# Fused convolution stack, KAN layer: two exponentials and six products a network, SiLU and variance root by ScalarE tables, one ring of bases, strided identity sum, another order

## The chip, the cores and the metric

One core of one Trainium2 chip runs the whole program in one launch. The metric is device time in microseconds. The program takes 10815.07 us (median of 3 runs, 10814.88 to 10825.75).

## The reference

Four layers are added to a tensor `x` of 8 x 32 x 256 x 256 f32, each on the group-normalized `x`: a hyperbolic convolution block, a spectral layer, a window layer of four KAN networks, and a local binary pattern. The change is in the third. Its reference, cut to what matters (`y` is the layer-normalized input; one set of 16 or 32 values is one row of a network):

```python
GRID, DENOM = jnp.linspace(-2.0, 2.0, 8), 4.0 / 7.0
def _fastkan(x, ln_g, ln_b, ws, wb, bb):
    ln = _layernorm(x, ln_g, ln_b)
    basis = jnp.exp(-((ln[..., None] - GRID) / DENOM) ** 2)      # 8 bases
    return basis.reshape(*basis.shape[:-2], -1) @ ws.T + jax.nn.silu(x) @ wb.T + bb
a = _fastkan(columns of windows of y, k1...)     # 16 values a row
d = _fastkan(rows of windows of y, k2...)        # 16 values a row
e = _fastkan(channels of y, k3...)               # 32 values a row
z = _fastkan(a + d + e, k4...)                   # 32 values a row
out = z + wins
```

## The kernel before

`build_program` runs the layers one after another; `window_layer` (from L1679) is the third, and `prepare_kan` prepares its constants. It works on 64 tiles of 128 partitions x 2048 f32, each half a band of eight rows of the images. The five normalizations are PN (of the input, L1991 and L1995 write `y`) and those of the networks K1 to K4.

A tile goes through these steps. Each normalization has three on TensorE, which share the four PSUM banks `norm`: `center` (L2115, L2118), `variance` (L2128, from the squares `sq`) and `spread` (L2139, which spreads the reciprocal roots). Between them ScalarE moves the centered values out of PSUM (L1863, L1865) and squares them (L1872), VectorE takes the variance (`take`, L1979) and works out the reciprocal root by a polynomial (`chain`, eight small steps in `rsqrt_polynomial`, L116 to L130; K1, K2 and K3 in one chain, PN and K4 in the other), and multiplies (`scale`, L1991).

A network's eight bases are exp(-(v + c - n)^2) up to a constant. ScalarE computes three of them (the anchors 0, 3 and 6) as a square (L1898, `args`) and an exponential (L1902, `exps`), and once a network the ratio exp(2v) (L1907, `ratio`). VectorE makes each of the other five from the base below it by one multiplication with the ratio (`grow`, L2042); the constant that is left over is multiplied into the weights `kan_basis`. Anchors lie in `ex` (three buffers), the others in `grown_ex` (three buffers). TensorE multiplies each base by its weights (`products`, L2180: 32 instructions, a matmul of f32 being two) and sums in the other four PSUM banks, `out`. Ahead of base 4 it adds the SiLU part (L2173), for K3 also the result of K1 through the identity (L2166), for K4 the residual (L2170). SiLU is x (1 + tanh(x/2)) / 2: Tanh on ScalarE (L1881, L1886), the rest on VectorE (L2000), the half in the weights.

`out` is evacuated by ScalarE for K1, K2 and K4 (L1912). For K3 VectorE adds `out`, the bias and the result of K2 into `z` (`total`, L2007); it reads `out` row by row while it lies column by column, and so with a stride. K1 and K2 get their inputs by DMA (`feed_y`, `feed_u`) and give back by DMA (`give_back`). For K2 the tile is first turned, columns first, by VectorE (`turn_y` L1958, `turn_u` L1963), with a stride of eight words on reading.

The order of the work is written out by hand: every step has a position (`CENTER`, `MOVE`, `GROW`, ... ), in units of which 128 make a round; position 168 is unit 40 of the round after the tile's own. Each engine goes through the units of all rounds and issues what is due, so that several tiles are in work at once, and waits on semaphores for what it needs. All rounds are unrolled. In a round the products of the networks come in the order K4, K1, K2, K3.

## Time and profile before

| | before |
|---|---|
| time, median of 3 runs | 10815.07 us |
| the profiled execution, its span | 10821.2 us |
| TensorE, VectorE, ScalarE busy, whole span | 8878.0, 8891.7, 8014.9 us |
| window layer, from the first `x` out of PSUM to the last `out` | 4403 to 10060 us |
| granted TensorE clock, mean | 0.936 |

The profiled execution's own time is its span, first to last instruction; no other time of it is given. The layers ahead of the window layer take about 4400 us, the one behind it about 750. A row of a group of instructions gives the busy time, the mean of one in ns, and behind the bar the idle time of the engine just before them with what ended it. Consecutive instructions overlap a little, so the start of the next one tells what one costs.

### The profile page before, as it was taken

How to read it: one execution, taken by the hardware profiler on the slowest of the kernel's cores; microseconds unless marked ns; L12 is line 12 of the kernel's file. 1: busy time of each engine (PE TensorE's matmuls, PEld its weight loads, DVE VectorE, ACT ScalarE, POOL GpSimd, SP SyncE). 2: the span in 40 equal slices, each digit the busy share in tenths (PEclk: the TensorE clock that was granted, in tenths of full speed). 3: DMA queues.
4: the chain of work that ended last, by engine and by line, in shares of the span. 5: the costliest groups of instructions: out<-in, count | busy, mean ns of one | idle time of the engine just before them, and what ended most of it. 6: DMA issues, size and time to landing. Idle time of an engine off the chain costs nothing. (4 is left out here: it accounts for less than half of the span.)

```text
span 10821.2 us, 354779 instructions
## 1 busy us (share of the span) xinstructions
PE 8878.0 (82%) x158376; PEld 4547.3 (42%) x158376; DVE 8891.7 (82%) x9022; ACT 8014.9 (74%) x5451; POOL 0.2 (0%) x4
## 2 busy tenths in 40 slices
PE   0889879996665799588888888888888888888788
PEld 0344434433442688244444444444344444443444
DVE  6777756666777588699999999999999999998788
ACT  0555545554552555599999999999999999998788
POOL 0000000000000000000000000000000000000000
PEclk9999989998887999699999999999999999999899
DMA  7999979996663588355444454555445455554576
GB/s 286 247 257 260 240 217 263 266 264 211 267 274 120 155 279 277 77 115 111 110 107 111 107 111 107 115 119 112 111 107 111 107 111 115 119 110 93 173 211 195
DMA packets 1196555, 1825.76 MB, mean 169 GB/s; under 512 B 135328, under 2 KB 956448, under 8 KB 1124768
## 3 DMA queue, kind: packets, MB, share of 16 engines
q1 hardware_dynamic: 1195040, 1803.05, 61.9%
q8 instruction: 1257, 20.59, 0.8%
q14 instruction: 258, 2.11, 0.1%
HBM read 717.78 MB, written 411.04 MB: 104 GB/s over the span
## 5 line engine op out<-in xcount | busy, mean ns | idle before, releaser
L2042 DVE SCALAR_TENSOR_TENSOR grown_ex<-ratio,ex 128x2048 f32<-128x2048 f32 x768 | 1756.1, 2287 | 229.7 <-PE out L2180 162.1
L2180 PE MATMUL out<-grown_ex,kan_basis 32*32 32x512 f32 x40960 | 1691.9, 625 | 7.7 <-DVE grown_ex L2042 5.4
L556 PE MATMUL conv<-uc,w 128*32 128x512 f32 x12288 | 1445.6, 596 | 15.4 <-DMA uc<-u 15.4
L1902 ACT ACTIVATE ex<-ex 128x2048 f32<-128x2048 f32 x768 | 1447.6, 1901 | 4.2
L2180 PE MATMUL out<-ex,kan_basis 32*32 32x512 f32 x24576 | 1233.3, 660 | 256.5 <-ACT ku L1912 156.5
L2042 DVE SCALAR_TENSOR_TENSOR grown_ex<-ratio,grown_ex 128x2048 f32<-128x2048 f32 x512 | 1171.2, 2288 | 27.4 <-PE out L2180 21.3
L463 ACT ACTIVATE v<-conv,cb 128x512 f32<-128x512 f32 x512 | 350.8, 685 | 899.6 <-PE conv L556 388.3
L2180 PEld LDWEIGHTS out<-grown_ex,kan_basis 32*32 32x32 f32 x40960 | 590.6, 106 | 731.1 <-issue 631.5
L1898 ACT ACTIVATE ex<-kin,offset 128x2048 f32<-128x2048 f32 x384 | 758.6, 1991 | 128.4 <-PE out L2180 127.8
L556 PEld LDWEIGHTS conv<-uc,w 128*32 128x32 f32 x12288 | 498.0, 109 | 715.7 <-issue 667.9
L2319 DVE TENSOR_TENSOR d<-xt 128x2313 f32<-128x2313 f32 (+2 forms) x256 | 621.7, 2495 | 88.2 <-PE acc L2373 87.9
L2373 PE MATMUL acc<-d,weights 32*32 32x512 f32 x16384 | 626.6, 599 | 73.3 <-issue 67.4
L2180 PEld LDWEIGHTS out<-ex,kan_basis 32*32 32x32 f32 x24576 | 419.6, 107 | 613.3 <-issue 532.5
L2139 PE MATMUL norm<-q,c_sel 32*128 32x128 f32 x10240 | 461.5, 328 | 171.5 <-ACT x L1863 136.6
L2139 PEld LDWEIGHTS norm<-q,c_sel 32*128 32x128 f32 x10240 | 391.8, 226 | 481.7 <-ACT x L1863 195.5
L2341 ACT ACTIVATE d<-d,steep 128x2313 f32<-128x2313 f32 (+2 forms) x256 | 534.0, 2159 | 35.3 <-DVE d L2319 35.3
L660 DVE TENSOR_TENSOR u<-xn,spread 128x512 f32<-128x512 f32 (+2 forms) x320 | 379.3, 1218 | 165.7 <-PE spread L521 163.5
L2128 PE MATMUL norm<-sq,c_kan_ones 128*32 128x128 f32 x10240 | 362.0, 281 | 176.3 <-ACT y L1865 76.0
L2173 PE MATMUL out<-ku,kan_silu 128*128 128x512 f32 x1024 | 472.6, 605 | 1.5 <-DVE grown_ex L2042 1.5
L2128 PEld LDWEIGHTS norm<-sq,c_kan_ones 128*32 128x32 f32 x10240 | 271.5, 112 | 464.8 <-issue 197.0
L2373 PEld LDWEIGHTS acc<-d,weights 32*32 32x32 f32 x16384 | 319.5, 103 | 327.7 <-issue 216.5
L1898 ACT ACTIVATE ex<-z,offset 128x2048 f32<-128x2048 f32 x192 | 383.2, 1996 | 54.5 <-PE out L2180 44.0
(287 smaller groups left out, 16012.2 us busy)
## 6 DMA issues: line engine op xcount, KB each, us to landing
uc<-u SPq DMA_DIRECT2D x2048, 129.0 KB, 3.5
xt<-in_x SPq DMA_DIRECT2D x128, 1024.0 KB, 7.3
t<-v SPq DMA_DIRECT2D x128, 1024.0 KB, 9.7
back_k<-ku SPq DMA_DIRECT2D x1024, 128.0 KB, 4.0
xt<-in_x SPq DMA_DIRECT2D x32, 2048.0 KB, 7.8
xt<-t SPq DMA_DIRECT2D x64, 1024.0 KB, 6.6
tt<-t SPq DMA_DIRECT2D x64, 1024.0 KB, 12.1
x<-x SPq DMA_DIRECT2D x64, 1024.0 KB, 4.9
```

What stands on the lines that cost most here:

```text
L556: last = m.matmul(conv[QUAD * b:QUAD * b + QUAD, k % 2, :], w_sb[:, o, d, :], uc[:, h, b, 2 * p:2 * p + 2, d:d + COLS], start=(d == 0), st ...
L660: return v.tensor_tensor(inside(u[:, h, first_row:first_row + rows, 1:COLS + 1]), inside(xn[:, h, at].rearrange("p (r w) -> p r w", w=COLS ...
L1898: a.activation(ex[:, j], norm_out(kind, h), ACT.Square, bias=k["offset"][:, kind - 1, n:n + 1]).then_inc(args, 1)
L1902: a.activation(ex[:, j], ex[:, j], ACT.Exp, scale=-1.0).then_inc(exps, 1)
L2042: v.scalar_tensor_tensor(grown_ex[:, at % GROWN], ratio[:], LARGEST, below, ALU.min, ALU.mult).then_inc(grown, 1)
L2128: last = m.matmul(norm[rows(quarter), 0, 0:P], k["c_kan_ones"][:, 0 if kind in (K1, K2) else 1, i, :], sq[:, block_:block_ + P], start=(i ...
L2139: last = m.matmul(norm[:, quarter, P * i:P * i + P], k["c_sel4"][rows(quarter), i, :], q[group][rows(quarter), group.index(kind), :], star ...
L2173: m.matmul(out[:, i, :], k["kan_silu"][:, kind - 1, :], silu_of(kind, h)[:, cols(i)], start=False, stop=False)
L2180: last = m.matmul(out[rows(i), g, :], k["kan_basis"][rows(g), kind - 1, n, :], base[rows(g), cols(i)], start=(n == 0), stop=(n == BASES - ...
L2319: v.tensor_tensor(d[:, h, n, rows, columns], there, xt[:, parity, h, rows, columns], ALU.subtract).then_inc(diff_ready, 1)
L2341: a.activation(t, t, ACT.Tanh, scale=steep[:, h:h + 1]).then_inc(tanh_ready, 1)
L2373: last = m.matmul(acc[quad(k), h, g, :], weights[quad(g), n, :], source_tile[quad(g), row + 2 * k:row + 2 * k + 2, column:column + COLS], ...
```

## The change

In the window layer alone:

- Two anchors a network, 0 and 4, instead of three; bases 1, 2, 3, 5, 6 and 7 come from products with the ratio, six instead of five.
- All eight bases of all networks go through one ring `ex` of six buffers, in order of use; a base may be written when the base six before it has been used by TensorE and the one above that has been made.
- SiLU by ScalarE's own function (`ACT.Silu`), whose table set is not that of the exponentials: `tables` loads a set where another one is active. VectorE's half of SiLU goes, and the factor one half in the weights.
- The reciprocal root as exp(-0.5 ln(v + eps)) on ScalarE, `log` reading the variance out of PSUM and `root` on 128 x 128 values, each network by itself. `take` and `chain` go.
- K2's result, not K1's, is added by the identity on TensorE, which reads it with a stride of 256 words; K1's result is added by VectorE at the evacuation of K3, which now reads `out` straight and writes `z` straight.
- SiLU(y) is turned by ScalarE (`TURN_U_BY_ACT`), the square of K3 goes to VectorE.
- Waits on constants in place of TensorE's counting registers; semaphores of `args`, `exps`, `ratios` and `grown` one for each network.
- Another order, in units of 256 to a round, with one round more of depth. The products come in the order K3, K1, K2, K4.

```diff
-ANCHORS = {K1: (0, 3, 6), K2: (0, 3, 6), K3: (0, 3, 6), K4: (0, 3, 6)}
-CHAINS = ((K1, K2, K3), (PN, K4))
-UNITS = 128
-STAGES = 4
+ANCHORS = (0, 4)
+GROWTHS = tuple(n for n in range(BASES) if n not in ANCHORS)
+EXP_SET, SILU_SET = "natural_log_exp_and_others", "silu_and_others"
+UNITS = 256
+CENTER = {PN: 437, K1: 727, K2: 749, K3: 732, K4: 1179}
+VARIANCE = {PN: 462, K1: 746, K2: 818, K3: 758, K4: 1216}
+SPREAD = {PN: 589, K1: 761, K2: 920, K3: 785, K4: 1223}
+EVACUATE = {K1: 922, K2: 1014, K3: 1040, K4: 1365}
+RATIO = {K1: 872, K2: 908, K3: 1065, K4: 1252}
+ANCHOR = {K1: (858, 875), K2: (883, 919), K3: (1060, 1099), K4: (1191, 1307)}
+EXP = {K1: (865, 877), K2: (888, 924), K3: (1063, 1112), K4: (1214, 1310)}
+PRODUCT = {K1: (921, 922, 938, 948, 950, 953, 959, 963),
+           K2: (985, 986, 987, 989, 993, 1003, 1007, 1008),
+           K3: (1115, 1124, 1125, 1128, 1135, 1136, 1144, 1165),
+           K4: (1274, 1286, 1288, 1296, 1299, 1300, 1301, 1305)}
+SILU = {PN: 617, K4: 1132}
+TURN_Y_BY_ACT = False
+TURN_U_BY_ACT = True
+SQUARED_BY_ACT = (PN, K1, K2, K4)
+STAGES = 5
+RING = 6
...
+        def base_buffer(kind, n, t):
+            return ex[:, serial(kind, n, t) % RING]
+        def buffer_free(eng, kind, n, t):
+            due = serial(kind, n, t) - RING
+            if due >= 0:
+                kind_before, t_before = slot_no.items[due // BASES]
+                n_before = due % BASES
+                eng.wait_ge(used, due + 1)
+                if n_before + 1 in GROWTHS:
+                    eng.wait_ge(grown[kind_before], len(GROWTHS) * t_before + GROWTHS.index(n_before + 1) + 1)
...
+            def tables(name):
+                if loaded_set[0] != name:
+                    a.preload_act_table_set(name)
+                    loaded_set[0] = name
...
-                    a.activation(U[:, h], Y[:, h], ACT.Tanh, scale=0.5).then_inc(tanh_ready[kind], 1)
+                    tables(SILU_SET)
+                    a.activation(U[:, t % 2], Y[:, t % 2], ACT.Silu).then_inc(u_ready[kind], 1)
...
+            def log(kind, t):
+                wait_past(act, spread_ready[kind], t)
+                act.wait_ge(var_ready[kind], t + 1)
+                tables(EXP_SET)
+                a.activation(logs[:, kind], norm[:, 0, 0:P], ACT.Ln, bias=k["eps"][:, 0:1],
+                             scale=1.0 * G / P if kind in (K1, K2) else 0.5 * G / P).then_inc(var_taken[kind], 1)
+            def root(kind, t):
+                act.wait_ge(var_taken[kind], t + 1)
+                tables(EXP_SET)
+                a.activation(roots[:, kind], logs[:, kind], ACT.Exp, scale=-0.5).then_inc(factors[kind], 1)
...
-                v.scalar_tensor_tensor(rows_first(Z[:]), rows_first(out_flat), out_b(K3, h), columns_first(D[:]), ALU.add,
-                                       ALU.add).then_inc(summed, 1)
+                    v.scalar_tensor_tensor(Z[:], out_flat, out_b(kind, t % 2), B[:], ALU.add, ALU.add).then_inc(evacuated[kind], 1)
...
-                            m.matmul(out[:, i, :], c["ident"][:], B[:, cols(i)], start=False, stop=False)
+                    by_rows = D[:].rearrange("p (x rw) -> p rw x", x=BAND)
+                    for i in range(CHUNKS):
+                        m.matmul(out[:, i, :], c["ident"][:], by_rows[:, BANK // BAND * i:BANK // BAND * i + BANK // BAND, :],
+                                 start=False, stop=False)
```

## Rows read from the trace of the kernel before

**Rows 1.** The page's first part: busy us, share of the span, instructions.

```profile
span 10821.2 us, 354779 instructions
PE 8878.0 (82%) x158376; PEld 4547.3 (42%) x158376; DVE 8891.7 (82%) x9022; ACT 8014.9 (74%) x5451; POOL 0.2 (0%) x4
```

**Rows 2.** Busy time in 46 tiles of the window layer; columns stand first.

```profile
core 0: us, PE busy (x) PEld busy (x) DVE busy (x) ACT busy (x) POOL busy (x), PEclk, DMA share, GB/s
5575.60:9564.80 3989.20, 3474.44 (x72495) 1645.45 (x72478) 3693.55 (x2622) 3698.72 (x1979) 0.00 (x0) 0.95 0.50 111
```

**Rows 3.** Tile `z`: times min/median/max in ns, first and last start.

```profile
L2007 DVE SCALAR_TENSOR_TENSOR z<-out,kan_vec,back_k x64: 3893/3946/3999, 4535.0 to 9998.1; 128x2048 f32<-128x2048 f32 x64
```

**Rows 4.** VectorE's groups in those 46 tiles: busy us, mean ns | idle before, releaser.

```profile
L2042 DVE SCALAR_TENSOR_TENSOR grown_ex<-ratio,ex 128x2048 f32<-128x2048 f32 x552 | 1262.1, 2286 | 149.6 <-PE out L2180 121.0 <-ACT ex L1902 19.9 <-issue 8.5
L2007 DVE SCALAR_TENSOR_TENSOR z<-out,kan_vec,back_k 128x2048 f32<-128x2048 f32 x46 | 181.7, 3950 | 20.7 <-ACT ex L1902 15.1 <-DMA back_k<-ku 5.6
L1991 DVE SCALAR_TENSOR_TENSOR z<-z,kan_vec,norm 128x2048 f32<-128x2048 f32 x46 | 107.8, 2344 | 0.1
L2000 DVE SCALAR_TENSOR_TENSOR silu_y<-silu_y,y 128x2048 f32<-128x2048 f32 x46 | 105.2, 2287 | 0.0
L1963 DVE COPY columns_first<-silu_y 128x2048 f32<-128x2048 f32 x46 | 93.5, 2033 | 0.0
L1979 DVE TENSOR_SCALAR q<-norm 128x128 f32<-128x128 f32 x230 | 65.7, 286 | 43.8 <-PE norm L2128 43.6
L120 DVE TENSOR_TENSOR t<-t,q 128x384 f32<-128x384 f32 x46 | 25.7, 559 | 3.4
L120 DVE TENSOR_TENSOR t<-t,q 128x256 f32<-128x256 f32 x46 | 19.6, 425 | 3.5
L116 DVE TENSOR_SCALAR rstd<-q 128x384 int32<-128x384 int32 x46 | 16.6, 360 | 4.3
L116 DVE TENSOR_SCALAR rstd<-q 128x256 int32<-128x256 int32 x46 | 13.5, 294 | 4.3
```

**Rows 5.** A tensor-tensor difference of the last layer, 2056 to 2313 elements, VectorE.

```profile
L2319 DVE TENSOR_TENSOR d<-xt x256: 2290/2558/2573, 10091.0 to 10800.9; 128x2313 f32<-128x2313 f32 x128
```

**Rows 6.** TensorE's groups in those 46 tiles.

```profile
L2180 PE MATMUL out<-ex,kan_basis 32*32 32x512 f32 x17663 | 885.2, 658 | 169.3 <-ACT ku L1912 110.2 <-ACT x_to_x L1912 50.0 <-issue 7.8
L2166 PE MATMUL out<-back_k,c_ident 128*128 128x512 f32 x368 | 174.4, 617 | 3.5 <-issue 3.5
```

**Rows 7.** One tile in order of time: start us, us; VectorE, then ScalarE.

```profile
6019.09 2.29 DVE L2042 SCALAR_TENSOR_TENSOR grown_ex<-ratio,grown_ex 128x2048 f32<-128x2048 f32 x1
6021.30 2.29 DVE L2042 SCALAR_TENSOR_TENSOR grown_ex<-ratio,ex 128x2048 f32<-128x2048 f32 x1
6023.50 2.03 DVE L1963 COPY columns_first<-silu_y 128x2048 f32<-128x2048 f32 x1
...
6020.00 1.92 ACT L1902 ACTIVATE ex<-ex 128x2048 f32<-128x2048 f32 x1
6021.82 1.98 ACT L1898 ACTIVATE ex<-kin,offset 128x2048 f32<-128x2048 f32 x1
6023.71 1.98 ACT L1907 ACTIVATE ratio<-kin,ratio_b 128x2048 f32<-128x2048 f32 x1
```

**Rows 8.** ScalarE in earlier layers: a table load, and passes over 128 elements.

```profile
3774.11 1.28 ACT L1311 ACT_TABLE_LOAD   x1
3775.40 0.91 ACT L1311 ACTIVATE grow<-z,w 128x256 f32<-128x256 f32 x2
...
L1155 ACT ACTIVATE xs<-rows,tables x128: 482/497/512, 3517.0 to 3706.2; 128x128 f32<-128x128 f32 x128
...
L805 ACT ACTIVATE th<-n x32: 293/297/309, 2603.3 to 3319.5; 128x128 f32<-128x128 f32 x32
```

More of the change, by code:

```diff
@@ L1785, in _, with rounds @@
+                t = self.number + (unit - position) // UNITS
+                return t if 0 <= t < TILES else None
+        def rounds(round_):
+            for n in range(TILES + STAGES):
+                round_(Round(n))
         @block.sync
@@ new lines, in exp, with growth @@
+            def exp(kind, j, t):
+                act.wait_ge(args[kind], len(ANCHORS) * t + j + 1)
+                tables(EXP_SET)
+                a.activation(base_buffer(kind, ANCHORS[j], t), base_buffer(kind, ANCHORS[j], t), ACT.Exp, scale=-1.0).then_inc(exps[kind], 1)
+            def growth(kind, t):
+                act.wait_ge(scaled[kind], t + 1)
+                last = slot_no.before(kind, t)
+                if last is not None:
+                    act.wait_ge(grown[last[0]], len(GROWTHS) * last[1] + len(GROWTHS))
+                tables(EXP_SET)
+                a.activation(ratio[:], norm_out(kind, t % 2), ACT.Exp, bias=k["ratio_b"][:, kind - 1:kind], scale=2.0).then_inc(ratios[kind], 1)
@@ L1914, in round_, with evacuate @@
+            def evacuate(kind, t):
+                act.wait_ge(used, serial(kind, BASES, t))
+                dst = R[:] if kind == K4 else silu_of(kind, t % 2)
+                a.activation(dst, out_flat, ACT.Identity, bias=out_b(kind, t % 2)).then_inc(evacuated[kind], 1)
             def round_(now):
@@ new lines, in round_ @@
+                    for kind in NORMS:
+                        if kind in MOVED_BY_ACT and (t := now.due(u, MOVE[kind])) is not None:
+                            move(kind, t)
+                        if kind in SQUARED_BY_ACT and (t := now.due(u, SQUARE[kind])) is not None:
+                            square(kind, t)
+                        if (t := now.due(u, LOG[kind])) is not None:
+                            log(kind, t)
+                        if (t := now.due(u, ROOT[kind])) is not None:
+                            root(kind, t)
@@ new lines, in round_ @@
+                    for kind in KANS:
+                        if (t := now.due(u, RATIO[kind])) is not None:
+                            growth(kind, t)
+                        for j in range(len(ANCHORS)):
+                            if (t := now.due(u, ANCHOR[kind][j])) is not None:
+                                anchor(kind, j, t)
+                            if (t := now.due(u, EXP[kind][j])) is not None:
+                                exp(kind, j, t)
+                        if kind in EVACUATED_BY_ACT and (t := now.due(u, EVACUATE[kind])) is not None:
+                            evacuate(kind, t)
@@ L1945, in _ @@
+            rounds(round_)
         @block.vector
@@ L2076, in _ @@
-            rounds(dve, round_)
+                    for kind in NORMS:
+                        if kind not in MOVED_BY_ACT and (t := now.due(u, MOVE[kind])) is not None:
+                            move(kind, t)
+                        if kind not in SQUARED_BY_ACT and (t := now.due(u, SQUARE[kind])) is not None:
+                            square(kind, t)
+                        if (t := now.due(u, SCALE[kind])) is not None:
+                            scale(kind, t)
+                    for kind in KANS:
+                        if kind not in EVACUATED_BY_ACT and (t := now.due(u, EVACUATE[kind])) is not None:
+                            evacuate(kind, t)
@@ new lines, in round_ @@
+                    for kind in KANS:
+                        for n in GROWTHS:
+                            if (t := now.due(u, GROW[kind][n])) is not None:
+                                grow(kind, n, t)
+                    for position, by_act, step in ((TURN_Y, TURN_Y_BY_ACT, turn_y), (TURN_U, TURN_U_BY_ACT, turn_u), (BETA, False, add_beta), (MEASURE, False, measure)):
+                        if not by_act and (t := now.due(u, position)) is not None:
+                            step(t)
@@ L2078, in _ @@
+            rounds(round_)
         @block.tensor
```

507 lines of the change are left out of this document (175 added, 332 removed).

## The prediction, made before the changed kernel was run

> **What bounds the kernel now.** I read the first part of the page, then the busy time by stretches, then one tile of the window layer engine by engine. The page gives a span of 10821.2 us with TensorE, VectorE and ScalarE busy 82, 82 and 74% [rows 1]; that is an average over unlike stages. The change touches only the window layer, so I need that layer's own period. `z` is written once for each of the 64 tiles, at 4535.0 us first and 9998.1 us last [rows 3], so one tile takes 5463.1 / 63 = 86.72 us and the layer is about half the span. I took 46 tiles from its middle, 3989.2 us [rows 2]: VectorE is busy 3693.55 / 46 = 80.3 us a tile, ScalarE 80.4, TensorE 75.5. No engine is the bound alone. They stand 6.4, 6.3 and 11.2 us a tile, in an order written out by hand, and all three carry nearly the same load. DMA is busy half the time, and no stretch of it ends many waits.
>
> VectorE's 6.4 us of gaps are of two kinds. The 16 small steps of the two reciprocal-root chains each have a gap of 3.4 / 46 = 0.07 us ahead of them [rows 4], 1.2 us in all, which belongs to the chains. The rest, 5.2 us, are true waits; half of them (121.0 / 46 = 2.6 us) stand before a product with the ratio and end when TensorE has used the base whose buffer is wanted [rows 4]. TensorE's largest waits are for the evacuation of `out`, the one set of banks for sums, by ScalarE: (110.2 + 50.0) / 46 = 3.5 us a tile [rows 6].
>
> Spans in these rows overlap a little. A product with the ratio lasts 2.29 us, but the next work starts 2.20 us after it; an exponential costs 1.82 us of the engine and a square with a bias 1.89 [rows 7]. I count these steps, not the durations.
>
> **VectorE, a tile.** Gone are: the chain of three networks, six steps of 0.56 and two of 0.36 us (4.1), the chain of two, six of 0.43 and two of 0.29 (3.1), their 1.2 us of gaps, five readings of the variance of 0.29 (1.4), the two half-SiLU products (2 x 2.20 = 4.4) and the turning of SiLU(y), which goes to ScalarE (2.03 less the overlap, 1.95) [rows 4]. The third network's evacuation read PSUM with a stride and took 3.95 us; now it reads straight, as the scaling does at 2.34, so 1.6 goes [rows 4]. Added are four products with the ratio, one more in each network (4 x 2.20 = 8.8), and the third network's square. The nearest row for that is a tensor-tensor difference of 2056 elements in 2.29 us, the shortest there [rows 5], so 2.2. Sum: -4.1 -3.1 -1.2 -1.4 -4.4 -1.95 -1.6 +8.8 +2.2 = -6.75. VectorE was occupied for 80.3 + 1.2 = 81.5 us and comes to 74.75.
>
> **ScalarE, a tile.** Four squares with a bias and four exponentials go: 4 x 1.89 + 4 x 1.82 = 14.8; the third network's square goes, 1.8. The two Tanh become two SiLU of the same size, taken at nothing; no row has a SiLU, and a row of Tanh on 128 elements has the same form of cost as the others, so I see no reason for a change either way. SiLU(y) is now turned here with a stride of eight words. Bounds: 1.8 us, a plain pass, and 1.8 times 1.69, the ratio of VectorE's strided to its straight reading of PSUM (3.95 to 2.34), so 3.0. I take 1.9, since VectorE's strided pass over SBUF [rows 4] is no dearer than its other full passes. Five logarithms and five exponentials of 128 elements are new. The nearest rows are 0.30 us (Tanh, no operand for scale or bias) and 0.49 us (two such operands) [rows 8]; ten of them are 3.0 to 4.9, less overlaps, and I take 3.5. Last, tables. The SiLUs want one set, exponentials and logarithms another. In a round's order on ScalarE (positions modulo 256) the first network's ratio stands at 104, SiLU(y) at 105, a square at 107, SiLU(z) at 108, the next exponential at 109: the two SiLUs stand together, and there is one pair of loads a tile. A load takes 1.28 us, and the next instruction starts right behind it [rows 8], so 2.6 us a tile, 166 us in all. Sum: 80.4 -14.8 -1.8 +1.9 +3.5 +2.6 = 71.8 us.
>
> Rows 8 show no gap behind the load. The Trainium skill (ScalarE: Activation LUTs, What ACT_TABLE_LOAD costs) puts a switch at about 2.66 us, a drain included. By that figure, an estimate, ScalarE would stand at 74.5 us a tile, and would still not be the most loaded engine.
>
> **TensorE, a tile.** The same products run. The registers that counted what to wait for go; gaps with no releaser shown before base products are under 0.3 us a tile [rows 6], so I take nothing for them. The sum with the identity, eight instructions of 0.6 us that overlap to 174.4 / 46 = 3.8 us a tile [rows 6], now reads its operand with a stride of 256 words between columns. Bounds: nothing, and the 1.69 above, +2.6 us; doubled it would be +3.8. Below nothing it can't go, the columns are the same. I take nothing, because VectorE reads SBUF with a stride without loss, and TensorE's pass over 512 f32 columns is slow enough for it (3.8 us for eight). So TensorE stays at 75.5 us and becomes the most loaded engine by 0.8 us.
>
> **Waits.** Anchors and products now share one ring of six buffers instead of three and three, so every base waits until the base six before it has been used. Behind a product that waits for this on VectorE stand all its other steps, the third network's evacuation and the scalings among them; behind an anchor on ScalarE, the evacuations for which TensorE waits. The number of buffers is the same, so I keep VectorE's 5.2 us of waits. That gives 74.75 + 5.2 = 80.0 us a tile. It leaves TensorE only 4.5 us of waits where it has 11.2. The new order puts two, one, three and two steps of the normalizations between one network's last product and the next network's first, where the old one has one, one, two and two, so there is more to hide an evacuation behind; still, variance, root and spreading of each network remain a relay over the same banks. If TensorE kept two thirds of its waits, it would ask for 75.5 + 7.5 = 83.0. I take 81.4, between the two. SyncE's queue has the same transfers, and a tile is still far longer than their issue.
>
> **Sum.** 64 x (86.72 - 81.4) = 340 us less. The third network's sums are finished 2.36 rounds behind the first centering instead of 2.02, so filling the pipeline may take 0 to 20 us more; I take 10. The profiled execution spans 10821.2 us, 6 us above the median of the runs; so 10821.2 - 340 + 10 - 6 = 10485.
>
> **The rivals.**
> A. TensorE takes over. All else is as above, but TensorE keeps most of its waits: at 84 to 86 us a tile the time is 10650 to 10780, with 85 about 10720. For it: TensorE's waits are for steps of one or two microseconds on the others, whose duration the change leaves. Against it: the other engines have 6 to 9 us less to do, and are ready sooner.
> B. Slower. TensorE keeps all its 11.2 us and the strided identity sum is dear: 75.5 + 11.2 + 2.6 = 89.3 us a tile, 10821.2 + 165 + 10 - 6 = 10990; doubled, 11067. It decides from the point at which the price of the stride and TensorE's waits together pass 11.2 us.
> The Trainium skill (Advanced Engine Details and Errata, SBUF Cachelines) speaks for B: successive accesses that fall on different 16-byte lines of SBUF pay a penalty, and here each column does; no row of this case shows it for TensorE.
> C. The ring frees VectorE. If its 2.6 us of waits for used bases go, it needs 77.4 us a tile: 10821.2 - 596 + 10 - 6 = 10229. Against it: TensorE would have 1.9 us of waits left. Halfway to the forecast it gives about 10340.
> D. The tables are not held: the set is changed at every logarithm and at every exponential behind one. Five pairs of loads more are 13 us, ScalarE comes to 84.8, with its present 6.3 us of waits to 91.1 us a tile, and the time to 11105.
>
> **How the numbers follow.** Forecast (80 to 83.5 us a tile, 10395 to 10620): 0.58. A: 0.18. B: 0.13. C: 0.07. D: 0.02. The remaining 0.02 is a time within 0.2% of now; 0.2% is about what a measurement of this kernel can tell from no change. Faster is the forecast, A and C, 0.83; the same 0.02; slower 0.15. The range runs from C's halfway point, 10340, to 10880, where B is well begun; it leaves out about 0.05 below and 0.12 above.
>
> **What would show it.** In the middle of the layer VectorE should be busy 74 to 75 us a tile, ScalarE 71 to 73, TensorE 75 to 77 at a like clock; 128 table loads; the identity sum near 0.6 us an instruction, against 1.0 or more under B; a period of 81.4 us. Waits of VectorE for used bases well under 2.6 us mean C; a TensorE busy 75.5 with over 8 us of waits, A. I should be wrong most easily in the waits, which I carry over from another order.

## The result, and the profile after

The changed kernel takes 11002.12 us (median of 4 runs, 10986.19 to 11035.08) against 10814.97 us (10807.23 to 10825.75) for the kernel before: a ratio of 1.0173, with an interval of 1.0150 to 1.0196. It is slower by 1.7%, where 3.1% faster was forecast (10485 us), and it lies outside the range given (10340 to 10880). Rival B had 10990.

The page's first part of the kernel after:

```profile
span 10991.8 us, 350519 instructions
PE 9088.7 (83%) x158376; PEld 4584.7 (42%) x158376; DVE 8630.6 (79%) x7794; ACT 7545.8 (69%) x5712; POOL 0.2 (0%) x4
```

Against [rows 1], VectorE is busy 261 us less and ScalarE 469 us less; only TensorE has more, 211 us, with the same number of matmuls. The span grew by 170.6 us. Tile `z` of the kernel after (duration ns min/median/max, first and last start):

```profile
L1996 DVE SCALAR_TENSOR_TENSOR z<-out,kan_vec,back_k x64: 2350/2352/2352, 4558.6 to 10192.6; 128x2048 f32<-128x2048 f32 x64
```

So a tile takes (10192.6 - 4558.6) / 63 = 89.43 us, 2.71 more than by [rows 3], and 63 x 2.71 = 171 us is the whole of the loss in the span. Outside of it things cancel: the first `z` starts 23.6 us later than in [rows 3], and what follows the last one is 23.9 us shorter. Busy time of the engines in the middle of the layer, in the columns of [rows 2]:

```profile
5536.80:9667.60 4130.80, 3623.49 (x72500) 1689.81 (x72500) 3509.94 (x1748) 3356.49 (x2164) 0.00 (x0) 0.95 0.56 108
```

A share of this stretch times the period gives an engine's busy time a tile, and the rest of the period is its waiting: TensorE 3623.49 / 4130.80 x 89.43 = 78.4 us busy and 11.0 waiting, VectorE 76.0 and 13.4, ScalarE 72.7 and 16.8. In the kernel before they were 75.5 and 11.2, 80.3 and 6.4, 80.4 and 6.3 [rows 2, 3]. What the change took from VectorE and ScalarE stands there as waiting. All the tables below are worked out in this way, from the first and last `z` and a middle stretch of each kernel.

TensorE's groups in that stretch (busy us, mean ns of one | idle us before, by releaser), in order of cost, some left out:

```profile
L2129 PE MATMUL out<-ex,kan_basis 32*32 32x512 f32 x47104 | 1838.8, 622 | 222.3 <-DVE ex L2008 90.1 <-DVE z L1996 56.6 <-issue 43.8
...
L2103 PE MATMUL out<-back_k,c_ident 128*128 128x512 f32 x368 | 329.2, 1049 | 0.0
L2090 PE MATMUL norm<-roots,c_sel 32*128 32x128 f32 x7364 | 293.6, 294 | 106.1 <-ACT logs L1885 74.3 <-issue 31.5 <-ACT roots L1891 0.2
L2080 PE MATMUL norm<-sq,c_kan_ones 128*32 128x128 f32 x7360 | 279.5, 295 | 138.9 <-DVE z L1984 114.1 <-issue 24.5
```

Two things are new against [rows 6]. The sum with the identity, which now reads its operand with a stride, has a mean of 1049 ns where it had 617, and takes 329.2 / 46 = 7.2 us of a tile where it took 3.8: +3.4 us. And "issue", waiting with no releaser, has grown. The waits of the matmuls for issue in the same stretch (us in total, times, longest):

```profile
PE out L2129 <- issue: 43.8, 25, 3.7
PE norm L2090 <- issue: 31.5, 20, 4.4
PE norm L2080 <- issue: 24.5, 10, 3.8
PE out L2110 <- issue: 3.8, 7, 0.9
```

All these gaps add up to 103.6 us in 46.2 tiles, 2.2 us a tile; the same view of the kernel before adds up to 28.9 us in 46, 0.6 a tile. The change of the period is then made up for TensorE as: strided sum +3.4, its other work -0.5, gaps with no releaser +1.6, waits that another engine ends 8.8 where they were 10.6, so -1.8; in sum +2.7.

VectorE and ScalarE in the same stretch: where VectorE waits now, the products with the ratio, the turning of SiLU(y), the new logarithms and roots, and the table loads.

```profile
L2008 DVE SCALAR_TENSOR_TENSOR ex<-ratio,ex 128x2048 f32<-128x2048 f32 x1104 | 2519.1, 2290 | 156.3 <-ACT ratio L1910 86.0 <-ACT ex L1902 46.4 <-PE out L2129 0.3
...
L1996 DVE SCALAR_TENSOR_TENSOR z<-out,kan_vec,back_k 128x2048 f32<-128x2048 f32 x46 | 108.2, 2351 | 212.5 <-PE out L2129 212.5
L1978 DVE TENSOR_TENSOR sq<-y 128x2048 f32<-128x2048 f32 x46 | 105.5, 2294 | 134.8 <-PE norm L2080 134.8
...
L1864 ACT ACTIVATE columns_first<-silu_y 128x2048 f32<-128x2048 f32 x46 | 185.6, 4034 | 0.0
...
L1835 ACT ACT_TABLE_LOAD x92 | 118.0, 1283 | 236.0 <-PE out L2129 235.2
...
L1885 ACT ACTIVATE logs<-norm,eps_ln 128x128 f32<-128x128 f32 x230 | 83.7, 364 | 178.4 <-PE norm L2080 174.9
L1891 ACT ACTIVATE roots<-logs 128x128 f32<-128x128 f32 x230 | 69.2, 301 | 2.9
```

VectorE now stands 212.5 / 46 = 4.6 us a tile for the third network's sums, and ScalarE 5.1 for the same sums ahead of its table load. The place in one tile, in order of time (start us, us; TensorE, then VectorE, then ScalarE):

```profile
7044.78 4.46 PE L2129 MATMUL out<-ex,kan_basis 32*32 32x512 f32 x128 [0.69 <-ACT x_to_x L1915]
7049.17 7.16 PE L2103 MATMUL out<-back_k,c_ident 128*128 128x512 f32 x8
7056.15 3.61 PE L2113 MATMUL out<-silu_y,kan_silu 128*128 128x512 f32 x8
7059.69 4.47 PE L2129 MATMUL out<-ex,kan_basis 32*32 32x512 f32 x128
...
7064.20 2.35 DVE L1996 SCALAR_TENSOR_TENSOR z<-out,kan_vec,back_k 128x2048 f32<-128x2048 f32 x1 [4.87 <-PE out L2129]
...
7061.01 1.28 ACT L1835 ACT_TABLE_LOAD   x1 [5.34 <-PE out L2129]
7062.31 1.91 ACT L1874 ACTIVATE silu_y<-y 128x2048 f32<-128x2048 f32 x1
...
7066.64 1.91 ACT L1879 ACTIVATE silu_z<-z 128x2048 f32<-128x2048 f32 x1 [0.53 <-DVE z L1996]
7068.57 1.28 ACT L1835 ACT_TABLE_LOAD   x1
```

TensorE goes from 7044.78 to 7064 without a gap, and the strided sum is 7.16 us of it; VectorE and ScalarE have run out of other work and stand 4.87 and 5.34 us. So here the strided sum lies bare on the path.

### The profile page after: what moved, and what is told of

Read it like the earlier page. It is cut to its first block and busy times, and to the rows that moved or that the text cites. A ratio compares the mean times of both kernels' runs of the same rounds, so it can differ in the third digit from the quotient of the medians.

```text
span 10991.8 us, 350519 instructions
## 1 busy us (share of the span) xinstructions
PE 9088.7 (83%) x158376; PEld 4584.7 (42%) x158376; DVE 8630.6 (79%) x7794; ACT 7545.8 (69%) x5712; POOL 0.2 (0%) x4
## 5 line engine op out<-in xcount | busy, mean ns | idle before, releaser
L2008 DVE SCALAR_TENSOR_TENSOR ex<-ratio,ex 128x2048 f32<-128x2048 f32 x1536 | 3504.4, 2290 | 226.7 <-ACT ratio L1910 134.7
L2129 PE MATMUL out<-ex,kan_basis 32*32 32x512 f32 x65536 | 2563.7, 624 | 321.8 <-DVE ex L2008 129.2
L2129 PEld LDWEIGHTS out<-ex,kan_basis 32*32 32x32 f32 x65536 | 1073.3, 105 | 1466.3 <-issue 801.5
L1902 ACT ACTIVATE ex<-ex 128x2048 f32<-128x2048 f32 x512 | 975.6, 1905 | 2.9
L2262 DVE TENSOR_TENSOR d<-xt 128x2313 f32<-128x2313 f32 (+2 forms) x256 | 621.7, 2494 | 83.3 <-PE acc L2316 82.9
L1896 ACT ACTIVATE ex<-kin,offset 128x2048 f32<-128x2048 f32 x256 | 511.3, 1997 | 130.5 <-PE out L2129 115.0
L2090 PE MATMUL norm<-roots,c_sel 32*128 32x128 f32 x10240 | 411.0, 296 | 152.1 <-ACT logs L1885 104.9
L660 DVE TENSOR_TENSOR u<-xn,spread 128x512 f32<-128x512 f32 (+2 forms) x320 | 379.1, 1218 | 170.6 <-PE spread L521 168.4
L2090 PEld LDWEIGHTS norm<-roots,c_sel 32*128 32x128 f32 x10240 | 342.7, 197 | 355.0 <-ACT logs L1885 202.5
L2103 PE MATMUL out<-back_k,c_ident 128*128 128x512 f32 x512 | 458.0, 1049 | 0.0
L1835 ACT ACT_TABLE_LOAD x133 | 170.6, 1283 | 352.0 <-PE out L2129 315.2
L513 PE MATMUL pc<-sqv,c_ones 128*32 128x256 f32 x2048 | 314.9, 380 | 91.0 <-ACT sqv L464 91.0
L1996 DVE SCALAR_TENSOR_TENSOR z<-out,kan_vec,back_k 128x2048 f32<-128x2048 f32 x64 | 150.5, 2351 | 305.0 <-PE out L2129 305.0
```

The source lines that it names most:

```text
L1896: a.activation(base_buffer(kind, ANCHORS[j], t), norm_out(kind, t % 2), ACT.Square, bias=k["offset"][:, kind - 1, ANCHORS[j]:ANCHORS[j] + ...
L1902: a.activation(base_buffer(kind, ANCHORS[j], t), base_buffer(kind, ANCHORS[j], t), ACT.Exp, scale=-1.0).then_inc(exps[kind], 1)
L2008: v.scalar_tensor_tensor(base_buffer(kind, n, t), ratio[:], LARGEST, base_buffer(kind, n - 1, t), ALU.min, ALU.mult).then_inc(grown[kind], 1)
L2090: last = m.matmul(norm[:, quarter, P * i:P * i + P], k["c_sel4"][rows(quarter), i, :], roots[rows(quarter), kind, :], start=(i == 0), stop ...
L2103: m.matmul(out[:, i, :], c["ident"][:], by_rows[:, BANK // BAND * i:BANK // BAND * i + BANK // BAND, :], start=False, stop=False)
L2129: last = m.matmul(out[rows(i), g, :], k["kan_basis"][rows(g), kind - 1, n, :], base[rows(g), cols(i)], start=(n == 0), stop=(n == BASES - ...
```

## The experiments

The table gives, a tile, the period, TensorE's busy time and waits, the part of its waits with no releaser, VectorE's waits, and the ratio to the kernel before on the same chip. Edits are to the kernel after unless the row says "before". The ratios compare runs on one chip; a difference in microseconds to the kernel after, given in the text, is one of medians from different chips, on which the kernel before itself took 10815 to 10834 us, so it is good to some 20 us. TensorE's busy time includes what the clock does; the granted clock in that stretch was 0.95 in most runs, 0.97 in e7, e8 and e10, 0.94 in e3, e5 and e11, 0.92 in e12.

| run | period us | TensorE busy / waits | no releaser | VectorE waits | ratio (95%) |
|---|---|---|---|---|---|
| before | 86.72 | 75.5 / 11.2 | 0.6 | 6.4 | 1 |
| after | 89.43 | 78.4 / 11.0 | 2.2 | 13.4 | 1.0173 (1.0150-1.0196) |
| e1 straight sum | 85.80 | 75.3 / 10.5 | 2.2 | 9.8 | 0.9953 (0.9938-0.9968) |
| e2 before, strided sum | 90.39 | 79.2 / 11.2 | 0.8 | 10.2 | 1.0217 (1.0200-1.0234) |
| e3 turn on VectorE | 92.54 | 79.8 / 12.7 | 2.1 | 14.6 | 1.0344 (1.0329-1.0360) |
| e4 square on ScalarE | 91.71 | 78.8 / 12.9 | 0.5 | 17.9 | 1.0280 (1.0259-1.0301) |
| e5 old sum | 87.15 | 75.9 / 11.2 | 1.9 | 9.5 | 1.0036 (1.0025-1.0048) |
| e6 no loads | 89.85 | 78.9 / 11.0 | 2.1 | 13.6 | 1.0169 (1.0153-1.0184) |
| e7 small transfers | 87.10 | 77.2 / 9.9 | 0.7 | 11.0 | 1.0019 (1.0010-1.0029) |
| e8 order | 89.68 | 78.0 / 11.7 | 2.2 | 13.6 | 1.0161 (1.0146-1.0176) |
| e9 before, short chain | 86.34 | 75.5 / 10.9 | 0.6 | 12.7 | 0.9967 (0.9955-0.9979) |
| e10 load earlier | 86.93 | 77.2 / 9.7 | 0.6 | 11.0 | 0.9996 (0.9986-1.0007) |
| e11 old sum, load earlier | 85.10 | 75.1 / 10.0 | 0.3 | 7.8 | 0.9893 (0.9874-0.9912) |
| e12 the same, square on ScalarE | 89.71 | 76.8 / 13.0 | 0.1 | 14.6 | 1.0169 (1.0153-1.0185) |

### The stride of the identity sum: e1, e2, e5

e1 lets the sum read `D` as it lies, so that the second network's result enters in a wrong order of columns; everything else stays.

```diff
-m.matmul(out[:, i, :], c["ident"][:], by_rows[:, BANK // BAND * i:BANK // BAND * i + BANK // BAND, :],
+m.matmul(out[:, i, :], c["ident"][:], D[:, cols(i)],
```

> The changed kernel, but the identity sum of K3 reads the tile D straight instead of with a stride of 256 words; the result of K2 is then added in the wrong order of columns, which is the part of the computation that this leaves out. In the changed kernel the eight instructions of that sum take 7.2 us a tile instead of 3.8. Theory S (the stride's 3.4 us lie on the path, because TensorE keeps its 11 us of waits a tile): a tile gets shorter by about 3.4 us, the kernel by about 215 us, to about 10785. Rival O (the order and the steps that changed engine set the period): the 3.4 us turn into waits of TensorE, and the time stays within 50 us of 11000.

Measured: 10778.14 us (10772.69 to 10798.69), 224 us less than the kernel after, as expected. The group of this sum in e1, in the same stretch:

```profile
L2103 PE MATMUL out<-back_k,c_ident 128*128 128x512 f32 x384 | 177.6, 605 | 0.0
```

1049 ns is 605 again, the sum's busy time falls from 7.2 to 177.6 / 48.1 = 3.7 us a tile, and the period by 3.6.

e2 is the opposite, in the kernel before: its sum reads `B` with the same stride, so that the first network's result enters in another order of columns, and nothing else changes.

```diff
+by_rows = B[:].rearrange("p (x rw) -> p rw x", x=BAND)
-m.matmul(out[:, i, :], c["ident"][:], B[:, cols(i)], start=False, stop=False)
+m.matmul(out[:, i, :], c["ident"][:], by_rows[:, BANK // BAND * i:BANK // BAND * i + BANK // BAND, :], start=False, stop=False)
```

> The kernel before, with one part of the change alone: the identity sum (there of K1's result) reads its tile with the stride of 256 words. The values are then added in the wrong order of columns, which is what it leaves out. Theory S: the sum's instructions go from 0.6 to 1.04 us, 3.4 us a tile, and TensorE's waits don't take them up: slower by 150 to 220 us, 10965 to 11035. Rival O: the 11.2 us of waits that TensorE has a tile take up most of it, slower by less than 70 us.

Measured: 11066.06 us, +236 us to the kernel before, 31 us above the range expected. The group in e2:

```profile
L2167 PE MATMUL out<-back_k,c_ident 128*128 128x512 f32 x360 | 323.3, 1053 | 0.3 <-issue 0.3
```

The period rises by 3.7 us, TensorE's busy time by 3.7, and its waits stay at 11.2: VectorE's and ScalarE's waits rise instead, by 3.8 each. Even the order before, in which the three engines looked equally loaded, passes on the whole of what is put on TensorE in this place.

e5 undoes this part of the change whole: the first network's result is added by the identity, straight, and the second's by VectorE in the strided evacuation (SyncE's waits ahead of the transfers to `B` and `D` are exchanged to match, which is not shown).

```diff
-dve.wait_ge(back_loaded[K1], 128 * t + 128)
-v.scalar_tensor_tensor(Z[:], out_flat, out_b(kind, t % 2), B[:], ALU.add, ALU.add)
+dve.wait_ge(back_loaded[K2], 128 * t + 128)
+v.scalar_tensor_tensor(rows_first(Z[:]), rows_first(out_flat), out_b(kind, t % 2), columns_first(D[:]), ALU.add, ALU.add)
...
-pe.wait_ge(back_loaded[K2], 128 * t + 128)
+pe.wait_ge(back_loaded[K1], 128 * t + 128)
...
-m.matmul(out[:, i, :], c["ident"][:], by_rows[:, BANK // BAND * i:BANK // BAND * i + BANK // BAND, :],
+m.matmul(out[:, i, :], c["ident"][:], B[:, cols(i)],
```

> The changed kernel with its strided sum undone in full, all else as changed: K1's result goes through the identity and is read straight, K2's result is added by VectorE, which reads PSUM with a stride (3.95 us instead of 2.35). The result is complete. Theory S: TensorE gains 3.4 us a tile and VectorE's evacuation, for which TensorE also waits, costs 1.6 more, so 1.8 to 3.4 us a tile are won: 10785 to 10890. Rival O: within 50 us of 11000, or slower.

Measured: 10874.85 us, 127 us less than after but 97 more than e1. VectorE's evacuation takes 3.93 us instead of 2.35, and TensorE's next product waits for it: 136.1 us in that stretch where it was 56.6, 1.7 us a tile more. Against e1 the period is 1.35 us longer: TensorE's waits in all grew by 0.7 (those for products with the ratio shrank, from 70.0 us in e1's stretch to 34.3), and its busy time by 0.6, at a granted clock of 0.94 for 0.95. So the change's trade was 1.6 us of VectorE, most of which comes back in the period, for 3.4 us of TensorE, all of which does.

### Is the load of VectorE and ScalarE on the path? e9, e6, e3

e9 leaves the polynomial out of the root chains of the kernel before (only the first guess of each root is left, so this part of the computation is changed), which is most of what the change took from VectorE, and nothing else.

```diff
-rsqrt_polynomial(v, y[:, 0:len(due)], q[group][:, some], t_[:, 0:len(due)], q[group][:, some]).then_inc(factors[group], 1)
+v.tensor_scalar(q[group][:, some].bitcast(I32), q[group][:, some].bitcast(I32), -0.5, 1597463007.0, ALU.mult, ALU.add).then_inc(factors[group], 1)
```

> The kernel before with VectorE's two reciprocal-root chains cut to their first step; the polynomial is left out, so the roots are rough. VectorE has about 7.3 us a tile less to do, as much as the change took from it, and the roots are ready 3.4 to 4.3 us earlier. Theory R (in such an order TensorE's stream with its relay of waits sets the period, and less load on another engine counts only where a relay gets shorter): less than 2.5 us a tile won, slower than 10660. Rival L (the load of VectorE and ScalarE sets the period in the old order, and the new order spoiled it): ScalarE at 80.4 us a tile still holds, so up to 5 us a tile, down to 10500.

Measured: 10802.22 us. VectorE is busy 80.3 - 73.6 = 6.7 us a tile less, all that the change was to save there, and the period falls by 0.4. Its groups in e9, the middle 46 tiles:

```profile
L2042 DVE SCALAR_TENSOR_TENSOR grown_ex<-ratio,ex 128x2048 f32<-128x2048 f32 x554 | 1266.4, 2286 | 350.2 <-PE out L2180 324.7 <-ACT ex L1902 25.4 <-issue 0.2
L1991 DVE SCALAR_TENSOR_TENSOR y<-x,kan_vec,norm 128x2048 f32<-128x2048 f32 x46 | 108.0, 2348 | 137.4 <-PE norm L2139 137.4
```

The waits for TensorE to use a base are 324.7 us where [rows 4] has 121.0, and a scaling waits 137.4 us: 4.4 and 3.0 us a tile, where the work was. VectorE's load does not set the period; its waits in [rows 4] are slack, not a price that comes with its work. ScalarE kept its 80.2 us in this run; what work taken from ScalarE alone would do in the kernel before, no run shows.

e6 puts an exponential and a square in the places of the two SiLUs (a changed part of the computation), so that no table is loaded in the layer; SiLU(y) is shown.

```diff
-tables(SILU_SET)
-a.activation(U[:, t % 2], Y[:, t % 2], ACT.Silu).then_inc(u_ready[kind], 1)
+tables(EXP_SET)
+a.activation(U[:, t % 2], Y[:, t % 2], ACT.Exp, scale=-1.0).then_inc(u_ready[kind], 1)
```

> The changed kernel with the two SiLUs replaced by functions of the exponentials' table set (an exponential and a square; the SiLU is left out), so that no table is loaded: ScalarE has 2.6 us a tile less. Theory R: one load stands right ahead of SiLU(y), behind a wait of 5 us, and the other right ahead of an exponential on which VectorE's products wait; 0.5 to 2 us a tile are won, 10870 to 10970. Rival (table loads are not on the path): within 25 us of 11000.

Measured: 11011.55 us, no less than after. ScalarE is busy 2.1 us a tile less and waits 2.5 more. The first of the two loads stands where ScalarE waits 5 us anyway, the second right behind SiLU(z) with no wait (7068.57 above); both together cost nothing here, and I had expected them to cost something.

e3 turns SiLU(y) on VectorE again.

```diff
-TURN_U_BY_ACT = True
+TURN_U_BY_ACT = False
```

> The changed kernel with SiLU(y) turned by VectorE again. On ScalarE that pass took 4.03 us, over twice what a straight one takes; on VectorE it takes 2.05. ScalarE has 4.0 us a tile less, VectorE 2.0 more. If ScalarE's queue is what the others wait for (rival A2: the pass delays the anchors behind it), a tile gains 1 to 4 us, 10750 to 10940. Theory S: neither engine is the bound, within 60 us of 11000.

Measured: 11201.03 us, 1.7% more than after by the two ratios, which I had not expected. ScalarE loses 3.7 us a tile of work, VectorE gains 1.9, and the period rises by 3.1. TensorE's products with bases in e3:

```profile
L2129 PE MATMUL out<-ex,kan_basis 32*32 32x512 f32 x45571 | 1803.3, 631 | 293.6 <-DVE ex L2008 169.9 <-DVE z L1996 53.8 <-issue 38.8
```

They wait 169.9 / 44.6 = 3.8 us a tile for VectorE's products where it was 2.0; TensorE's waits are 1.7 us longer in all. The other 1.4 us of the 3.1 are its own busy time, at a granted clock of 0.94 for 0.95. The turning stands ahead of products with the ratio in VectorE's order. That a step of 2 us added in one place costs 3, and 6.7 us taken away in other places bring 0.4 (e9), says that it is not the sum of VectorE's work that counts here, but what it puts ahead of a product that TensorE waits for.

### The order of single steps: e8, e4

e8 moves the first network's evacuation and two products of the second network a little earlier.

```diff
-EVACUATE = {K1: 922, K2: 1014, K3: 1040, K4: 1365}
+EVACUATE = {K1: 918, K2: 1014, K3: 1040, K4: 1365}
...
-           K2: (985, 986, 987, 989, 993, 1003, 1007, 1008),
+           K2: (968, 969, 987, 989, 993, 1003, 1007, 1008),
```

> The changed kernel with three positions of its order altered, no work changed: ScalarE evacuates K1 ahead of anchor 4 of K2 and the square of PN instead of behind them (3.7 us earlier), and TensorE does the first two products of K2 ahead of the variance of PN, where it waits 2.5 us a tile for VectorE's scaling. Theory R: TensorE's waits there are filled with work, 1 to 3 us a tile, 10800 to 10940. Rival: the waits turn up elsewhere, within 30 us of 11000.

Measured: 11007.29 us, nothing gained. TensorE waits 0.7 us a tile more and the wait has only moved: among what its base products wait for is now ScalarE's evacuation `ku`, 49.7 us in the stretch.

e4 gives the third network's square back to ScalarE.

```diff
-SQUARE = {PN: 408, K1: 677, K2: 805, K3: 685, K4: 1141}
+SQUARE = {PN: 408, K1: 677, K2: 805, K3: 696, K4: 1141}
...
-SQUARED_BY_ACT = (PN, K1, K2, K4)
+SQUARED_BY_ACT = (PN, K1, K2, K3, K4)
```

> The changed kernel with the square of K3 on ScalarE again, right behind K3's move out of PSUM. VectorE waits 2.9 us a tile for the buffer of the squares ahead of this step, and with the step itself that keeps the products with the ratio behind it back by 5 us; TensorE waits 2.0 us a tile for such products. Theory R: if those waits of TensorE shrink, 0.5 to 2 us a tile are won, 10870 to 10970. Rival: ScalarE, which then waits for the buffer, holds back its own steps, and the time is within 40 us of 11000 or above.

Measured: 11136.27 us, 1.1% more than after by the two ratios. ScalarE's square, VectorE's products with the ratio and TensorE's centering in e4:

```profile
L1854 ACT ACTIVATE sq<-y 128x2048 f32<-128x2048 f32 x45 | 86.0, 1912 | 173.1 <-PE norm L2080 173.1
...
L2008 DVE SCALAR_TENSOR_TENSOR ex<-ratio,ex 128x2048 f32<-128x2048 f32 x1079 | 2460.6, 2290 | 535.1 <-ACT ratio L1910 492.3 <-ACT ex L1902 11.3 <-issue 11.1
...
L2070 PE MATMUL norm<-kin,c_center 32*32 32x512 f32 x2880 | 159.3, 913 | 178.2 <-ACT logs L1885 178.2
```

The square waits 173.1 / 45 = 3.8 us for TensorE to have used the last `sq`, and everything behind it on ScalarE waits too: VectorE stands 492.3 / 45 = 10.9 us a tile for a ratio. TensorE's waits for VectorE's products stay as they were (87.6 / 45 = 1.9 us a tile); what it waits for more is ScalarE's logarithms, 178.2 / 45 = 4.0 us a tile where the kernel after has 35.7 / 46 = 0.8. The position 696 was my choice and only one was tried, so the run shows the price of a waiting instruction there, not that the square can't stand on ScalarE at all. VectorE has a wait of 2.9 us ahead of the same square in the kernel after.

### The gaps with no releaser: e7, e10

They come about once a tile, most of them in one phase of it (one ends at 6928.57, the next at 7019.06 us, 90.5 us on), while SyncE issues one transfer after another. SyncE's queue in one tile of the kernel after, then of e10 (start us, us of the run of issues, their number):

```profile
7000.89 6.29 SPq L1794 DMA_DIRECT2D kin<-columns_first  x8
7007.28 2.34 SPq L1783 DMA_DIRECT2D x_to_x<-x  x4
7009.72 18.66 SPq L1810 DMA_DIRECT2D back_k<-ku  x16
7028.49 7.72 SPq L1801 DMA_DIRECT2D ku<-silu_y  x8
```

```profile
7025.70 1.74 SPq L1783 DMA_DIRECT2D x_to_x<-x  x4
7035.58 6.85 SPq L1794 DMA_DIRECT2D kin<-columns_first  x8
7042.53 17.51 SPq L1810 DMA_DIRECT2D back_k<-ku  x16
7060.14 6.45 SPq L1801 DMA_DIRECT2D ku<-silu_y  x8
```

In the kernel after 36 transfers go out in a row for 35.3 us, and the gap of this tile lies in them:

```profile
7019.06 2.02 PE L2129 MATMUL out<-ex,kan_basis 32*32 32x512 f32 x32 [3.70 <-issue]
```

e7 halves the bytes of the transfers that reshape `kin` and give a result back; the other half of these values stays zero, so it is left out of the computation. The transfer to `kin` is shown.

```diff
-sp.dma_start(kin[:, kind - K1, COLS * i:COLS * i + COLS],
-             src[P // G * i:P // G * i + P // G].rearrange("p (z n) -> p z n", z=BAND)).then_inc(kin_loaded[kind], 16)
+sp.dma_start(kin[:, kind - K1, COLS * i:COLS * i + 128],
+             src[P // G * i:P // G * i + P // G].rearrange("p (z n) -> p z n", z=BAND)[:, :, 0:128]).then_inc(kin_loaded[kind], 16)
```

> The changed kernel with the transfers that feed y to K1 and K2 and those that give back moving half their bytes (128 of every 256 words; half of those values are left out). TensorE has 2.3 us a tile of gaps with no releaser shown, once a tile, in the 35 us in which SyncE issues forty transfers in a row. Theory F (its instruction stream is fetched late because of these bursts): the gaps shrink by half or more, and the kernel gets faster by 60 to 150 us. Rival: the gaps stay as they are, and the time within 30 us.

Measured: 10844.97 us, 157 us less than after, a little more than expected. The engines' work is untouched; the DMA share falls from 0.56 to 0.42, the gaps from 2.2 to 0.7 us a tile, and TensorE's busy time from 78.4 to 77.2, with a granted clock of 0.97 for 0.95.

e10 leaves every byte and moves one load, that of the residual (four transfers), four positions of the hand-written order earlier.

```diff
-LOAD_X, LOAD_R, STORE = 168, 1009, 1203
+LOAD_X, LOAD_R, STORE = 168, 1005, 1203
```

> The changed kernel with one position altered: SyncE issues the four transfers of the residual (1 MB a tile) ahead of K2's input instead of behind it, in a stretch in which its queue is idle, so that they are not part of the burst in which TensorE's unexplained gaps lie. All bytes move. Theory F: the gaps (2.3 us a tile) shrink by a third to a half, 50 to 120 us won. Rival: the number of transfers sets the gaps, not their crowding, within 25 us of 11000.

Measured: 10827.92 us (10 runs, 10807.53 to 10850.60), 174 us less than after, from one number, where 50 to 120 had been expected. The load now goes out ahead of the run, which has 32 transfers. TensorE's waits for issue in e10:

```profile
PE out L2129 <- issue: 10.1, 14, 1.6
PE norm L2090 <- issue: 8.5, 7, 2.0
PE norm L2080 <- issue: 5.9, 9, 1.2
PE out L2110 <- issue: 3.3, 8, 0.5
...
```

With two more of 0.5 us together, 103.6 us have become 28.3, the level of the kernel before, with the same bytes and a DMA share of 0.58. Busy time in the stretch of e10:

```profile
5536.80:9667.60 4130.80, 3668.28 (x74736) 1716.80 (x74739) 3609.91 (x1804) 3451.32 (x2231) 0.00 (x0) 0.97 0.58 111
```

The period is 2.5 us shorter: 1.6 by the gaps and 1.2 by TensorE's busy time (78.4 to 77.2, at a granted clock of 0.97 for 0.95, as in e7), less 0.3 of other waits. So in this order the gaps answer to the transfers, to their bytes in e7 and to their place in e10.

That crowding is the cause isn't shown, and two kernels speak against it as the whole cause. The kernel before issues 41 transfers in a row, with the loads of the input and the residual and the store among them, from 7021.64 to 7053.07 us in one of its tiles, and has 0.6 us of gaps a tile:

```profile
7021.64 5.15 SPq L1812 DMA_DIRECT2D kin<-columns_first  x8
...
7051.08 1.99 SPq L1801 DMA_DIRECT2D x_to_x<-x  x4
```

And e4 has the same order on SyncE as the kernel after and only 0.5 us of gaps, in a tile with 3.7 us of other waits more. Perhaps a late instruction costs nothing where the engine would wait anyway. That TensorE's instructions come late because they share the way with the transfers is a guess, and no run settles it.

### The better version: e11, e12

e11 is e5 with the residual's load moved as in e10; the evacuation and SyncE's waits are edited as in e5.

```diff
-LOAD_X, LOAD_R, STORE = 168, 1009, 1203
+LOAD_X, LOAD_R, STORE = 168, 1005, 1203
...
-pe.wait_ge(back_loaded[K2], 128 * t + 128)
+pe.wait_ge(back_loaded[K1], 128 * t + 128)
...
-m.matmul(out[:, i, :], c["ident"][:], by_rows[:, BANK // BAND * i:BANK // BAND * i + BANK // BAND, :],
+m.matmul(out[:, i, :], c["ident"][:], B[:, cols(i)],
```

> The changed kernel with the strided sum undone (as in the run of the old sum, 10875) and the residual's transfers issued earlier. The result is complete. If the two add up: 10760 to 10830, about level with the kernel before. Rival (they don't add, TensorE's waits elsewhere grow): 10850 to 10890.

Measured: 10718.33 us (10712.37 to 10731.15), a ratio of 0.9893 (0.9874 to 0.9912) to the kernel before and 284 us less than after; 10760 to 10830 had been expected, before e10's gain was known. Busy time in its stretch:

```profile
5536.80:9667.60 4130.80, 3643.91 (x76184) 1790.26 (x76152) 3754.51 (x1837) 3520.48 (x2272) 0.00 (x0) 0.94 0.58 113
```

TensorE is busy 75.1 us and waits 10.0, of which 139.2 / 48.5 = 2.9 are for the strided evacuation of `z`. This is the fastest kernel of this study.

e12 is e11 with the third network's square on ScalarE at 696, as in e4.

```diff
-SQUARED_BY_ACT = (PN, K1, K2, K4)
+SQUARED_BY_ACT = (PN, K1, K2, K3, K4)
```

> As the run before, and the square of K3 on ScalarE. If VectorE's queue, now 1.6 us a tile fuller by the strided evacuation, is what TensorE waits for: 10680 to 10790, faster than the kernel before. Rival: 10790 to 10880.

Measured: 11015.17 us, far outside both ranges expected. The price of that position is not tied to the strided sum: the period rises by 4.6 us, 3.0 of TensorE's waits and 1.7 of its busy time at a clock of 0.92 for 0.94, where in e4 it rose by 2.3.

## Why the prediction was wrong

**The bound.** "No engine is the bound alone" was read from busy shares. e2 and e9 show otherwise for the same kernel: 3.7 us more on TensorE is 3.7 us of period, 6.7 us less on VectorE is 0.4. In the kernel before VectorE's load does not set the period, and work added to TensorE does in full; the same work taken from TensorE in the kernel after (e1) comes back in full too. The step that failed is the one named Waits, where I kept VectorE's 5.2 us and let TensorE's shrink from 11.2 to the 5.9 that 81.4 leaves. It was the other way round: TensorE has 11.0, and VectorE's rose to 13.4. Rival A kept most of TensorE's waits and B all of them; they had 0.31 together. A's reason, that TensorE's waits are for steps whose duration the change leaves, isn't borne out: the evacuation `ku`, 110.2 us of them in [rows 6], no longer holds TensorE, and in the kernel after it waits for VectorE's products, the scalings, the logarithms and for no releaser at all. The sum stayed and the parts changed, so that 11.0 comes so near 11.2 is partly chance.

**The price of the stride.** "I take nothing" was the second failed step. The instruction's median is 1040 ns, the sum costs 3.4 us a tile between the 2.6 and 3.8 of the upper bounds, and e1 and e2 show all of it in the time, 224 and 236 us. The row I leaned on, VectorE's strided copy, was of another engine, and I misread it. "VectorE reads SBUF with a stride without loss" compared that copy, 2.03 us, with passes that read two tensors, 2.29 us. A straight pass of VectorE that reads one tensor of the same size takes 1.29 us in both kernels; in the kernel after:

```profile
L1989 DVE TENSOR_SCALAR y<-y,kan_vec 128x2048 f32<-128x2048 f32 x46 | 59.2, 1287 | 1.6
```

It adds a constant where the other copies, and no straight copy of this size is in the trace, so the price of the stride on VectorE stays open; that there is none isn't shown. The Trainium skill (Advanced Engine Details and Errata, SBUF Cachelines) says that accesses on different 16-byte lines pay. TensorE's rows agree: 1.04 us against 0.59 (median) for the same 512 columns. The page gives no size for it.

**The miss in numbers.** The period came out 8.0 us over the forecast: 2.9 by TensorE's busy time (3.4 for the stride, less 0.5 of other work) and 5.1 by its waits (11.0 for 5.9). Of the waits that another engine ends, 10.6 us became 8.8: the order or the lighter engines did help, by 1.8, a third of the 5.3 that I took. The rest is the 1.6 us of gaps with no releaser. "SyncE's queue has the same transfers, and a tile is still far longer than their issue" was true in sum, but when they go out matters: moving four of them gave 174 us (e10), of which the gaps are 1.6 us a tile, about 100 us. Why the new order has these gaps and the old one has not stays open.

**Rival B** gave 89.3 us a tile and 10990 us; 89.43 and 11002 were measured. The mechanism was right, but the fit of the second digit is partly luck: the stride was dearer by 0.8 than its 2.6, the other work 0.5 less, and its 11.2 us of waits were 8.8 of the kind it meant and 2.2 of a kind it did not know.

**What held.** VectorE: 74.75 forecast, 76.0 measured (five products in a row took 11.47 us from 7068.72, so 2.30 from one start to the next, where I counted 2.20). ScalarE: 71.8 and 72.7. There the strided turn was mis-sized, 4.03 us for 1.9 (its bound of 3.0 was too low), which the rest of the sum made up for in part: logarithms and roots cost (83.7 + 69.2) / 46 = 3.3 us a tile for my 3.5, the loads 2.6, the SiLUs 1.91 us for Tanh's 1.90, all about as taken; some 1 us of what made up for it I can't name. The third network's square took 2.29 us for 2.2, its evacuation 2.35 for 2.34. The Trainium skill (ScalarE: Activation LUTs, What ACT_TABLE_LOAD costs) adds a drain to each switch; the trace does not show it: the load that begins at 7061.01 and takes 1.28 us is followed by the SiLU at 7062.31, and the load at 7068.57 begins as SiLU(z) ends, with the next exponential at 7069.86. Rival D did not occur: 92 loads in 46 tiles. Rival C came true by half, and its sign misled: VectorE's waits for used bases went from 2.6 us a tile to nothing (0.3 us in the whole stretch, L2008), which I had called the mark of C, but its other waits grew to more than these, 4.6 us a tile for the sums ahead of `z` and 134.8 / 46 = 2.9 ahead of the square. So the ring wasn't what held VectorE, against the reason given for keeping its 5.2 us. Filling took 23.6 us where I took 10, and the end gave it back, which I had not reckoned. The point halfway between C and the forecast is 10357 us, not 10340.

**What would have come of it.** With the stride alone away (e1) the change is worth 0.5%, with the load moved too and the old sum 1.1% (e11). An estimate for both at once, with the straight evacuation, is e1's 85.80 less e10's 2.5, so 83.3 us, or 83.8 with the 2.0 that the moved load gave in e11; it was not run, since it needs a column order that the straight sum does not have.

## What to carry to other kernels

Before adding up busy times on engines that look equally loaded, ask which one keeps its waits when work is taken from the others. Here TensorE kept 9.7 to 13.0 us of waits a tile in every run, whatever VectorE and ScalarE had to do, and some 3.5 us put on it or taken from it moved the period by as much (e2, e1), while the others' work counted only in the places on which TensorE waited. That a relay through shared PSUM banks keeps these waits is argued from what the engines wait for; no run changed the banks. Price a changed access pattern by a row of the same engine and the same kind of pass, and where there is none, take the dear bound when that engine is the one whose waits stay. And look where a moved transfer lands in its queue, even if their number and bytes are the same.

## What the runs showed of the hardware

- A matmul of 512 f32 columns that reads its moving operand with a stride of 256 words takes 1.04 us for 0.59 (medians, e1 and e2 confirm both ways). VectorE's strided copy of 2048 elements takes 2.07 us, between the 1.29 of a straight pass that reads one tensor and the 2.29 of one that reads two. Its sum of PSUM and SBUF takes 3.93 us with the PSUM operand and the result strided, for 2.35 with all straight (e5).
- ScalarE's pass over 2048 elements with a stride of eight words takes 4.03 us where its straight passes take 1.9: twice.
- A table load of 1.28 us has the next instruction right behind it, and taking both out of each tile left the time where it was (e6), on an engine that waits 16.8 us a tile.
- TensorE can have gaps that no semaphore explains, about 2 us a tile in the kernel after, where 36 transfers go out in a row; four of them moved ahead of the run, or half the bytes in the transfers that reshape, take most of them away (e10, e7). The kernel before sends 41 in a row and has 0.6 us, so the run alone doesn't make them.
